# Attention on GpSimd and ScalarE: three small jobs of VectorE moved to other engines

## The chip, the cores and the metric

One Trainium2 chip, one core. The metric is the device time of one execution in microseconds, the median of the runs.

## The reference

A transformer block with adaptive layer norms on x of 8 batches x 512 tokens x 256, all in float32:

```
mod = (silu(c) @ wmod).reshape(8, 6, 1, 256);  sa, ca, ga, sb, cb, gb = mod[:, 0..5]
h = layernorm(x) * (1 + ca) + sa
Q = h @ Wq.T (16 heads of 16);  latent_k = h @ Wk_down.T;  latent_v = h @ Wv_down.T (64 wide)
logits = (Q q_to_latent) latent_k / 8, causal;  attn = softmax(logits)
x = x + ga * ((attn latent_v) v_up @ Wout.T)
h = layernorm(x) * (1 + cb) + sb
x = x + gb * (mixture of 16 experts, each on its 512 best tokens, + a shared expert)(h)
```

(ga and gb are first pushed to a magnitude of at least 0.25.) The change is in the attention half alone.

## The kernel before, in words

All five engines run programs of their own, written out by hand, and meet through semaphores. A product in float32 is made of three float32r products: each operand is split into an upper half (a rounded copy, names ending in h) and a lower half (the operand less the upper half, names ending in l).

The attention stage goes through 8 batches of 2 units each (NU = 16, unit u = 2b + c holds 8 heads of batch b), and each unit through 8 steps k, one per head. In step k of unit u TensorE makes a pair: the scores of head k of unit u into LB (main, L646, the matmuls of L656), interleaved with the scores of head k of unit u+1 into MB (maxima, L621, L633), which serve only to find the row maxima. VectorE reduces MB to row maxima NM (maxima, L1329, L1337), four blocks a head; TensorE may overwrite a block of MB only when VectorE has read it. ScalarE takes the exponentials P of LB in two parts (main, L1032 and L1034), and TensorE may overwrite LB only after them. GpSimd masks the diagonal of P (main, L1863). TensorE multiplies P with V (pv, L694) four heads at a time, in steps 4 and 5 for the first half of the unit and in steps 0 and 1 of the next unit for the second.

The negative maxima must be in place before the main scores of the same heads: they ride as two more rows of QS. In step 0 (for the upper four heads of unit u) and step 4 (for the lower four of unit u+1) TensorE transposes NM (put_max, L643), ScalarE copies it twice with a factor of -1, to NMh and NMf (put_max, L1010), VectorE subtracts NMl = NMf - NMh, 16x128 (put_max, L1341, semaphore d_nm), and ScalarE in step 1 or 5, behind its exponentials of that step and its copy of the PV result (store_heads, L1040), waits for d_nm and issues two DMAs that put NMh and NMl into QS (store_max, L1018, L1024).

Beside this, in fixed steps of the same loops, runs the work of other batches:

- the next batches' norm and projections. VectorE takes the statistics of batch b+2 (stats1, L1297, in step 0 of an odd unit) and the moments (moments, L1288: four aggregations, then var + eps and -mean, L1294 and L1295, on 128x4), GpSimd the power -1/2 and a product (moments, L1842, L1844 and L1846), ScalarE the scaled rows xh (scale1), TensorE their transpose (hT, steps 5 and 6), ScalarE hf = the shifted and scaled transpose (hT, L980, steps 5 and 6), VectorE the upper half hh (hT, L1316, cast of 128x512, steps 6 and 7), GpSimd the lower half hl (hT, L1853: one at the end of step 7, one before the mask of step 0 of the next unit). TensorE projects q and k from hh and hl in steps 1, 2, 6 and 7 of the even unit (qk, L577), ScalarE writes the upper and VectorE the lower half of the result (L996, L1326), and v in steps 2 and 3 of the odd unit.
- the finished batches. Batch b-1's (in even units b-2's second half) output projection on TensorE (outproj, L598), its product with the gate on VectorE (L1357) and its sum with X on GpSimd (outproj, L1882: end of step 7 of the odd unit, and behind the mask of step 0 of the even unit); then the second norm of batch b-2: statistics and moments on VectorE (stats2, moments2, steps 1 and 2 of the even unit), power on GpSimd (step 2), th on ScalarE (scale2, steps 3 and 4), two products and sums on GpSimd (shift2, L1891 and L1893, steps 4 and 6), transposes and score products.

In GpSimd's loop (L1915) the work of a step stands behind its mask. hf is a single buffer, which ScalarE refills only when hl is done (hl_done); the output projection in step 7 of the odd unit uses the bank of PSUM that the second hf of step 6 has to leave first.

Of the kernel before, what the change touches and what calls it, by code (L numbers as in the profile page):

```python
# [13 lines left out]
NB = 8  # L14
# [4 lines left out]
NU = 16  # L19
# [44 lines left out]
def block_program(nc, x, wq, wkd, wvd, q2l, vup, wo, gate, uw, ub, gw, gb, dw, db, sg, su, sd, ct, wmod,  # L64
# [55 lines left out]
    h2 = at("h2", 81024, [128, 2, 2, 512], F32R)  # L120
    halfc = at("halfc", 89216, [128, 4])
    st2, mv2 = at("st2", 89248, [128, 4, 6]), at("mv2", 89344, [128, 4, 2])
    rs2, nm2 = at("rs2", 89376, [128, 4]), at("nm2", 89408, [128, 4])
    for i_, n_ in enumerate(("wq", "wk", "wv")):
# [107 lines left out]
    a_sil, a_ht, a_cut, a_xt, a_score = (sem(n) for n in ("a_sil", "a_ht", "a_cut", "a_xt", "a_score"))  # L232
    a_sd, a_sc6 = sem("a_sd"), sem("a_sc6")

    (d_s, d_w, d_modT, d_mod, d_gate, d_mv1, d_hh, d_st, d_mx, d_nm, d_rec, d_tf, d_mv2, d_h2, d_lg) = (sem(n) for n in (
        "d_s", "d_w", "d_modT", "d_mod", "d_gate", "d_mv1", "d_hh", "d_st", "d_mx", "d_nm", "d_rec", "d_tf", "d_mv2",
        "d_h2", "d_lg"))
# [7 lines left out]
        "g_ks", "g_fill", "g_rs1", "g_P", "g_nf", "g_hn", "g_x2", "g_rs2", "g_h2", "g_ht"))  # L245
    g_sd = sem("g_sd")

# [723 lines left out]
    def scalar_program(e):  # L971
# [8 lines left out]
        def hT(b, c, name):  # L980
# [29 lines left out]
        def put_max(u, half):  # L1010
            e.wait_ge(p_mt, 2 * u + half + 1)
            if u:
                e.wait_ge(d_nm, 2 * u + half - 1)
                e.wait_ge(c_nm[half], 32 * u)
            e.activation(NMh[half][:], MB[0:16, 1280:1408], ACT.Copy, scale=-1.0)
            e.activation(NMf[half][:], MB[0:16, 1280:1408], ACT.Copy, scale=-1.0).then_inc(a_nm, 1)

        def store_max(u, half):  # L1018
            base = 64 * (u % 2)
            e.wait_ge(d_nm, 2 * u + half + 1)  # L1020
            if u >= 2:
# [123 lines left out]
        vproj(0, 1, "p1")  # L1145
        hT(1, 0, "p0")
        hT(1, 1, "p1")
        put_max(0, 0)
        store_max(0, 0)

        for u in range(NU):
            b, odd = u // 2, u % 2
            new, new2, old, old2 = b + 1 < NB, b + 2 < NB, 1 <= b, 2 <= b
            for k in range(8):
# [23 lines left out]
                else:  # L1178
# [94 lines left out]
    def vector_program(e):  # L1273
# [13 lines left out]

        def moments(stt, mvt, rst, nmt, done):  # L1288
# [12 lines left out]
        def moments1(b):  # L1301
            if b:
                e.wait_ge(a_xh, 2 * b)
            moments(st, mv, rs, nm1, d_mv1)

        def split_weight(n, src):
# [7 lines left out]
            e.tensor_tensor(l_, src, h_.bitcast(F32), ALU.subtract).then_inc(d_w, 1)  # L1314

        def hT(b, c):  # L1316
            e.wait_ge(a_hf, 2 * b + c + 1)
            if b:
                e.wait_ge(p_v, 2 * b)
            e.tensor_copy(hh[:, c, :], hf[:, c, :]).then_inc(d_hh, 1)  # L1320

# [7 lines left out]
        def maxima(u, k):  # L1329
            n = n_head(u, k)  # L1330
            for bank, blocks in ((2, (1,)), (1, (2, 0)), (0, (3,))):
# [7 lines left out]
                m.then_inc(d_mx, 1)  # L1339

        def put_max(u, half):  # L1341
            e.wait_ge(a_nm, 2 * u + half + 1)
            if u:
                e.wait_ge(c_nm[half], 32 * u)
            e.tensor_tensor(NMl[half][:], NMf[half][:], NMh[half][:].bitcast(F32), ALU.subtract).then_inc(d_nm, 1)

# [17 lines left out]
        def moments2(b):  # L1364
            if b:
                e.wait_ge(a_th, 2 * b)
            moments(st2, mv2, rs2, nm2, d_mv2)

# [90 lines left out]
        for c in range(2):  # L1459
            hT(0, c)  # L1460
            e.wait_ge(d_hh, c + 1)
            e.tensor_tensor(hl[:, c, :], hf[:, c, :], hh[:, c, :].bitcast(F32), ALU.subtract).then_inc(hl_done, 1)
# [10 lines left out]
        for k in range(8):  # L1473
            maxima(0, k)
            if k == 4:
                put_max(0, 0)
            if k in (4, 5):
                hT(1, k - 4)

        for u in range(NU):  # L1480
            b, odd = u // 2, u % 2
            new, new2, old, old2 = b + 1 < NB, b + 2 < NB, 1 <= b, 2 <= b
            for k in range(8):
                if u + 1 < NU:
                    maxima(u + 1, k)
                if k == 0:
                    put_max(u, 1)
                if k == 4 and u + 1 < NU:
                    put_max(u + 1, 0)

# [16 lines left out]
                else:  # L1507
# [324 lines left out]
    def pool_program(e):  # L1832
# [8 lines left out]

        def moments(b, ready, rst, nmt, done):  # L1842
# [41 lines left out]
        def shift2(b, half):  # L1884
# [8 lines left out]
            e.tensor_tensor(H2[:, ks, :], th[:, ks, :], BT[b % 2][:, 1:2, :].broadcast_to([128, 2, D]), ALU.add).then_inc(g_h2, 1)  # L1893

        kept(e.memset(halfc[:], -0.5))
        settled()
# [7 lines left out]
        settled()  # L1904
        moments(0, d_mv1, rs, nm1, g_rs1)

# [3 lines left out]
        m.then_inc(g_fill, 1)  # L1910
        moments(1, d_mv1, rs, nm1, g_rs1)
        hT(1, 0)
        hT(1, 1)

        for u in range(NU):  # L1915
            b, odd = u // 2, u % 2
            new2, old, old2 = b + 2 < NB, 1 <= b, 2 <= b
            for k in range(8):
                if not odd and k == 0 and 2 <= b + 1 < NB:

                    hT(b + 1, 1)
                main(u, k)
                if not odd:
# [150 lines left out]
```

## Time and profile before

| | us |
|---|---|
| median of 3 runs | 1156.96 (1151.46 to 1160.07) |
| the profiled execution | 1156.82 |
| its span | 1155.1 |
| TensorE's granted clock over the span | 0.978 |

Times in rows are microseconds from the start of the span unless marked ns. PE is TensorE, PEld its weight loads, DVE VectorE, ACT ScalarE, POOL GpSimd, SP SyncE; ACTq is a DMA issue in ScalarE's queue. A row of the timeline gives start, duration, engine, line, operation, out<-in, shape, count of merged instructions, and in brackets the idle time of the engine before it with what ended it. A duration reaches beyond the start of the next instruction, since an engine works in a pipeline; the step from start to start is what an instruction costs its engine.

### The profile page before, as it was taken

To read this page: it belongs to the slowest core of one execution; us is meant where nothing else is said; L and a number is where in the kernel's file an instruction comes from. 1 tells how busy PE (TensorE), PEld (TensorE's weight loads), DVE (VectorE), ACT (ScalarE), POOL (GpSimd) and SP (SyncE) were. 2 spreads that over 40 slices of the span, in tenths; PEclk is the share of its full clock that TensorE was granted. 3 is DMA by queue.
4 is the path that set the end of the run, shared out by engine and by line. 5 is a ranking of instruction groups with operands and counts; after the bars stand their busy time and mean duration, and the time that the engine had idled before them with its cause. 6 is when DMAs were issued, how large, how long until landed. Compare 5 with 4: busy or idle time off the path is not lost.

```text
span 1155.1 us, 21701 instructions
## 1 busy us (share of the span) xinstructions
PE 1112.3 (96%) x7482; PEld 865.4 (75%) x7482; DVE 861.1 (75%) x2213; ACT 594.1 (51%) x1083; POOL 633.1 (55%) x669
## 2 busy tenths in 40 slices
PE   9899999999999989999799999999999999999996
PEld 4555556656656668888688888888888888888886
DVE  4787888898898679889877677676777767777552
ACT  2356767877877653222253444544445444455441
POOL 4134566676675552232356656566565655666644
PEclk9789989999999999999999999999999999999998
DMA  7544557777767644876346554555545555455621
GB/s 198 91 99 101 115 120 182 178 147 179 187 131 177 208 160 109 270 220 164 98 139 165 134 131 123 155 140 134 134 127 153 134 143 136 119 152 132 168 58 19
DMA packets 100333, 165.44 MB, mean 143 GB/s; under 512 B 18424, under 2 KB 65016, under 8 KB 98176
## 3 DMA queue, kind: packets, MB, share of 16 engines
q1 hardware_dynamic: 83360, 137.04, 43.5%
q0 software_dynamic: 14336, 25.70, 11.5%
q10 hardware_dynamic: 2528, 1.32, 0.7%
q8 instruction: 60, 0.98, 0.4%
q14 instruction: 49, 0.40, 0.1%
HBM read 103.71 MB, written 34.11 MB: 119 GB/s over the span
## 4 chain that ended last, share of the span: by engine, by line
PE 63%; DVE 11%; issue 8%; POOL 8%; ACT 5%; DMA 3%; ACTq 1%; SPq 0%; DVEq 0%; POOLq 0%
PE MB L564 14%; PE LB L564 13%; PE LB L882 8%; PE MB L882 8%; PE UB L694 4%; PE LB L656 4%; PE UB L564 3%; PE XB L564 3%; POOL out_y L2001 3%; DVE junk L1337 2%; PE MB L633 2%; POOL XG L1966 1%; ACT P L1032 1%; ACT P L1034 1%; POOL HTl L1959 1%
## 5 line engine op out<-in xcount | busy, mean ns | idle before, releaser
L1959 POOL TENSOR_TENSOR HTl<-HF,HTh 128x512 fp32r<-128x512 f32 x156 | 217.6, 1401 | 207.7 <-ACT HTh L1095 207.4
L1337 DVE CUSTOM_DVE_ANT_0 junk<-MB,MK 128x256 bf16<-128x256 f32 (+3 forms) x512 | 218.6, 482 | 36.4 <-PE MB L633 35.5
L1863 POOL TENSOR_SCALAR_AFFINE_SELECT P<-P 128x256 f32<-128x256 f32 x256 | 101.3, 420 | 138.9 <-ACT P L1034 138.9
L2001 POOL DMA_INDIRECT out_y<-EO,IDX x64 | 108.7, 1699 | 75.7 <-DVE EO L1819 65.7
L1106 ACT ACTIVATE SIL<-LB,gbT 128x512 f32<-128x512 f32 x64 | 43.9, 686 | 191.8 <-PE LB L564 188.7
L1032 ACT ACTIVATE P<-LB 128x768 f32<-128x768 f32 x128 | 103.9, 812 | 73.4 <-PE LB L656 70.3
L633 PE MATMUL MB<-KS,QS 48*128 48x256 f32 (+3 forms) x512 | 132.8, 368 | 5.2 <-DVE NM L1337 3.4
L1095 ACT ACTIVATE HTh<-HF 128x512 fp32r<-128x512 f32 x156 | 97.8, 628 | 72.2 <-DVE HF L1709 72.2
L656 PE MATMUL LB<-QS,KS 50*128 50x256 f32 (+3 forms) x512 | 124.9, 358 | 3.5 <-ACT P L1032 2.6
L656 PEld LDWEIGHTS LB<-QS,KS 50*128 50x128 f32 x512 | 78.9, 190 | 50.2 <-issue 33.4
L633 PEld LDWEIGHTS MB<-KS,QS 48*128 48x128 f32 x512 | 81.7, 195 | 19.0 <-DVE NM L1337 12.7
L882 PE MATMUL LB<-WDh,HTh 128*128 128x256 f32 x320 | 93.3, 291 | 2.4 <-DVE tb L1723 2.3
L1709 DVE SCALAR_TENSOR_TENSOR HF<-MB,ubT,SIL 128x512 f32<-128x512 f32 x64 | 47.7, 745 | 63.8 <-PE MB L564 28.8
L1682 DVE TENSOR_TENSOR OH<-R,iotab 128x1024 bf16<-128x1024 bf16 x64 | 94.6, 1481 | 0.0
L882 PE MATMUL MB<-WDh,HTh 128*128 128x256 f32 x320 | 91.4, 286 | 0.0
L694 PE MATMUL UB<-P,V 128*32 128x512 f32 (+3 forms) x1024 | 86.5, 457 | 4.6 <-POOL P L1863 4.3
L882 PE MATMUL MB<-WDl,HTh 128*128 128x256 f32 x320 | 90.5, 283 | 0.0
L882 PE MATMUL MB<-WDh,HTl 128*128 128x256 f32 x320 | 90.5, 283 | 0.0
L882 PE MATMUL LB<-WDh,HTl 128*128 128x256 f32 x320 | 90.4, 282 | 0.0
L882 PE MATMUL LB<-WDl,HTh 128*128 128x256 f32 x320 | 90.3, 282 | 0.0
L1709 DVE SCALAR_TENSOR_TENSOR HF<-LB,ubT,SIL 128x512 f32<-128x512 f32 x64 | 47.7, 745 | 51.1 <-PE LB L564 47.0
L1966 POOL DMA_INDIRECT XG<-tab,IDX x64 | 63.8, 996 | 37.3 <-DVE IDX L1692 22.8
(316 smaller groups left out, 3028.1 us busy)
## 6 DMA issues: line engine op xcount, KB each, us to landing
WR<-in_gw SPq DMA_DIRECT2D x16, 1024.0 KB
WR<-in_uw SPq DMA_DIRECT2D x16, 1024.0 KB
WR<-in_dw SPq DMA_DIRECT2D x16, 1024.0 KB
QS<-ST SPq DMA_DIRECT2D x96, 128.0 KB, 3.7
KS<-ST SPq DMA_DIRECT2D x90, 128.0 KB, 4.6
hD<-h SPq DMA_DIRECT2D x8, 1024.0 KB, 6.1
XT<-hD SPq DMA_DIRECT2D x7, 1024.0 KB, 8.3
X<-in_x SPq DMA_DIRECT2D x8, 512.0 KB, 5.2
```

The lines of the kernel that those rows point to most:

```text
L564: m = e.matmul(ps, a(c), r(c), start=(i == 0), stop=(i == 5))
L633: m = e.matmul(MB[:, o:o + w], QS[base:base + 48, k, i * 128:(i + 1) * 128], KS[base:base + 48, k, 0:w], start=True, stop=True)
L656: m = e.matmul(LB[:, o:o + w], KS[base:base + 50, k, j * 128:(j + 1) * 128], QS[base:base + 50, k, 128 * j:512], start=True, stop=True)
L694: m = e.matmul(UB[32 * h:32 * h + 32, 128 * j:512], V[b % 2][:, j, 8 * c + 4 * g + h, :], P[(8 * u + 4 * g + h) % NP][:, o:o + w], start=( ...
L882: m = e.matmul(ps, a[:, slots[f], ts], r[:, f, :], start=(f == 0 and t_ == 0), stop=(f == len(slots) - 1 and t_ == 2), skip_group_check=True)
L1032: e.activation(P[n % NP][:, 512:1280], LB[:, 512:1280], ACT.Exp).then_inc(a_p, 1)
L1095: e.activation(HTh[:, slot, :], hf_of(n)[:], ACT.Copy).then_inc(a_ht, 1)
L1337: m = e.tensor_tensor_reduce(junk[:, o:o + w], MB[:, o:o + w], MK[:, 512 - w:512], 1.0, -3e38, ALU.add, ALU.max, NM[:, k // 4, 4 * (k % 4) ...
L1709: e.scalar_tensor_tensor(out=hf_of(n)[:], in0=up, scalar=bias, in1=sil_of(n)[:], op0=ALU.add, op1=ALU.mult).then_inc(d_hf, 1)
L1863: m = e.affine_select(out=dd, in_=dd, compare_op=ALU.is_ge, fill=0.0, base=0, pattern=[[0, 2], [1, 128]], channel_multiplier=-1)
L1959: e.tensor_tensor(HTl[:, slot, :], hf_of(n)[:], HTh[:, slot, :].bitcast(F32), ALU.subtract).then_inc(g_ht, 1)
L2001: e.indirect_dma_start(out=out2, out_offset=bass.IndirectOffsetOnAxis(ap=IDX[x_ % 3][:, q:q + 1], axis=0), in_=EO[:, q, :], in_offset=None ...
```

## The change

Three jobs leave VectorE's program:

- NMl = NMf - NMh (put_max) goes to GpSimd, with semaphore g_nm in place of d_nm. GpSimd does it at the head of step 1 (upper heads of unit u) and step 5 (lower heads of unit u+1), before the mask of that step, and for the first time behind the two hl of batch 1. ScalarE's store_max stays where it is, in steps 1 and 5, and now waits for g_nm.
- The upper half hh of the next h (hT) goes to ScalarE as a Copy activation (upper, semaphore a_hh), in steps 6 and 7 of odd units behind hf. Batch 0 keeps its cast on VectorE.
- The two small operations at the end of moments go to GpSimd's moments, as a product of the mean with a tile of -1 and a sum of the variance with a tile of eps, in front of the power. VectorE signals behind its last aggregation. For the last batch's second norm VectorE's own form stays.

```diff
         def upper(b, c):
+            e.wait_ge(a_hf, 2 * b + c + 1)
+            e.wait_ge(p_v, 2 * b)
+            e.activation(hh[:, c, :], hf[:, c, :], ACT.Copy).then_inc(a_hh, 1)
...
 scalar put_max / store_max
-                e.wait_ge(d_nm, 2 * u + half - 1)
+                e.wait_ge(g_nm, 2 * u + half - 1)
...
-            e.wait_ge(d_nm, 2 * u + half + 1)
+            e.wait_ge(g_nm, 2 * u + half + 1)
...
         hT(1, 0, "p0")
+        upper(1, 0)
         hT(1, 1, "p1")
+        upper(1, 1)
...
                     if k in (5, 6) and new2:
                         hT(b + 2, k - 5, ("hTa", "hTb")[k - 5])
+                    if k in (6, 7) and new2:
+                        upper(b + 2, k - 6)
...
 vector moments
-            kept(m)
-            settled()
-            e.tensor_scalar(rst[:], mvt[:, :, 1], EPS, None, ALU.add)
-            e.tensor_scalar(nmt[:], mvt[:, :, 0], -1.0, None, ALU.mult).then_inc(done, 1)
+            m.then_inc(done, 1)
...
 vector loops
-                if k == 0:
-                    put_max(u, 1)
-                if k == 4 and u + 1 < NU:
-                    put_max(u + 1, 0)
...
-                    if k in (6, 7) and new2:
-                        hT(b + 2, k - 6)
...
 gpsimd moments
+            e.tensor_tensor(nmt[:], mvt[:, :, 0], minus[:], ALU.mult)
+            kept(e.tensor_tensor(rst[:], mvt[:, :, 1], epsc[:], ALU.add))
+            settled()
             kept(e.tensor_tensor(rst[:], rst[:], halfc[:], ALU.pow))
...
 gpsimd hT
-            e.wait_ge(d_hh, 2 * b + c + 1)
+            e.wait_ge(a_hh, 2 * (b - 1) + c + 1)
...
+        def put_max(u, half):
+            e.wait_ge(a_nm, 2 * u + half + 1)
+            if u:
+                e.wait_ge(c_nm[half], 32 * u)
+            e.tensor_tensor(NMl[half][:], NMf[half][:], NMh[half][:].bitcast(F32), ALU.subtract).then_inc(g_nm, 1)
...
         hT(1, 0)
         hT(1, 1)
+        put_max(0, 0)
...
                 if not odd and k == 0 and 2 <= b + 1 < NB:
                     hT(b + 1, 1)
+                if k == 1:
+                    put_max(u, 1)
+                if k == 5 and u + 1 < NU:
+                    put_max(u + 1, 0)
                 main(u, k)
```

## Rows read from the trace of the kernel before

**Rows 1.** Busy time, share of the span and instructions of each engine.

```profile
PE 1112.3 (96%) x7482; PEld 865.4 (75%) x7482; DVE 861.1 (75%) x2213; ACT 594.1 (51%) x1083; POOL 633.1 (55%) x669
```

**Rows 2.** Stretches: bounds, length, busy time per engine, clock, DMA share, GB/s.

```profile
0.00:430.00 430.00, 405.81 (x2964) 249.16 (x2965) 345.54 (x1357) 284.42 (x543) 240.57 (x383) 0.95 0.62 150
...
212.64:256.74 44.10, 42.97 (x356) 27.10 (x356) 38.93 (x167) 34.02 (x66) 29.72 (x49) 1.00 0.73 167
```

**Rows 3.** Timeline of TensorE: first instruction of three pairs, and what follows each.

```profile
214.65 0.38 PE L656 MATMUL LB<-QS,KS 50*128 50x256 f32 x1
...
216.07 0.38 PE L564 MATMUL UB<-wvh,hh 128*128 128x256 f32 x1
...
240.32 0.38 PE L656 MATMUL LB<-QS,KS 50*128 50x256 f32 x1
...
241.54 0.73 PE L564 MATMUL XB<-h,GPh 128*128 128x512 f32 x2
...
250.46 0.38 PE L656 MATMUL LB<-QS,KS 50*128 50x256 f32 x1
...
251.30 0.51 PE L564 MATMUL XB<-hh,wkh 128*128 128x512 f32 x1
```

**Rows 4.** Groups by line from 75 to 410 us: busy, mean ns, idle before.

```profile
L1345 DVE TENSOR_TENSOR NMl<-NMf,NMh 16x128 fp32r<-16x128 f32 x29 | 13.5, 465 | 10.0 <-ACT NMf L1016 8.8
...
L1047 ACT ACTIVATE HNh<-nf 128x512 fp32r<-128x512 f32 x14 | 9.0, 642 | 1.1 <-POOL nf L1873 1.1
...
L1320 DVE CAST hh<-hf 128x512 fp32r<-128x512 f32 x12 | 5.1, 425 | 1.1 <-ACT hf L986 1.1
```

**Rows 5.** Timeline of VectorE, one batch.

```profile
234.18 0.72 DVE L1345 TENSOR_TENSOR NMl<-NMf,NMh 16x128 fp32r<-16x128 f32 x1
...
238.07 0.75 DVE L1285 BATCH_NORM_STATS2 st<-X 128x6 f32<-128x256 f32 x2 [0.26 <-POOL X L1882]
...
238.74 0.67 DVE L1326 SCALAR_TENSOR_TENSOR ST<-XB,ST 128x512 fp32r<-128x512 f32 x1
...
255.63 0.51 DVE L1345 TENSOR_TENSOR NMl<-NMf,NMh 16x128 fp32r<-16x128 f32 x1 [0.57 <-ACT NMf L1016]
```

**Rows 6.** Timeline of GpSimd, one batch.

```profile
231.41 0.77 POOL L1863 TENSOR_SCALAR_AFFINE_SELECT P<-P 128x256 f32<-128x256 f32 x2 [1.09 <-ACT P L1034]
...
232.23 1.28 POOL L1882 TENSOR_TENSOR X<-X,tf 128x512 f32<-128x512 f32 x1
...
233.48 2.57 POOL L1855 TENSOR_TENSOR hl<-hf,hh 128x512 fp32r<-128x512 f32 x2
...
236.74 1.30 POOL L1882 TENSOR_TENSOR X<-X,tf 128x512 f32<-128x512 f32 x1
...
242.80 0.20 POOL L1846 TENSOR_TENSOR nm<-nm,rs 128x4 f32<-128x4 f32 x1
...
246.17 1.29 POOL L1891 TENSOR_TENSOR th<-th,BT 128x512 f32<-128x512 f32 x1
...
247.54 1.28 POOL L1893 TENSOR_TENSOR H<-th,BT 128x512 f32<-128x512 f32 x1
```

**Rows 7.** Timeline of ScalarE, with its DMA issues, one batch.

```profile
226.05 1.36 ACTq L1024 DMA_DIRECT2D QS<-NMl  x1
...
229.36 0.79 ACT L986 ACTIVATE hf<-XB,modT 128x512 f32<-128x512 f32 x1
...
236.48 0.51 ACTq L1024 DMA_DIRECT2D QS<-NMh  x1
...
238.54 0.81 ACT L1032 ACTIVATE P<-LB 128x768 f32<-128x768 f32 x1
...
248.00 0.51 ACTq L1024 DMA_DIRECT2D QS<-NMh  x1
...
249.26 0.81 ACT L1032 ACTIVATE P<-LB 128x768 f32<-128x768 f32 x1 [0.64 <-PE LB L656]
```

**Rows 8.** The tile NMl: its DMAs from issue to landing.

```profile
DMA to landing us min/median/max: 1.9/2.8/5.6
```

More of the change, by code:

```diff
@@ L120, in block_program @@
     h2 = at("h2", 81024, [128, 2, 2, 512], F32R)
-    halfc = at("halfc", 89216, [128, 4])
+    halves, shifts = at("halves", 89216, [128, 8]), at("shifts", 89408, [128, 8])
+    halfc, minus = halves[:, 0:4], halves[:, 4:8]
+    nm2, epsc = shifts[:, 0:4], shifts[:, 4:8]
     st2, mv2 = at("st2", 89248, [128, 4, 6]), at("mv2", 89344, [128, 4, 2])
-    rs2, nm2 = at("rs2", 89376, [128, 4]), at("nm2", 89408, [128, 4])
+    rs2 = at("rs2", 89376, [128, 4])
     for i_, n_ in enumerate(("wq", "wk", "wv")):
@@ L232, in block_program @@
     a_sil, a_ht, a_cut, a_xt, a_score = (sem(n) for n in ("a_sil", "a_ht", "a_cut", "a_xt", "a_score"))
-    a_sd, a_sc6 = sem("a_sd"), sem("a_sc6")
-    (d_s, d_w, d_modT, d_mod, d_gate, d_mv1, d_hh, d_st, d_mx, d_nm, d_rec, d_tf, d_mv2, d_h2, d_lg) = (sem(n) for n in (
-        "d_s", "d_w", "d_modT", "d_mod", "d_gate", "d_mv1", "d_hh", "d_st", "d_mx", "d_nm", "d_rec", "d_tf", "d_mv2",
+    a_sd, a_sc6, a_hh = sem("a_sd"), sem("a_sc6"), sem("a_hh")
+    (d_s, d_w, d_modT, d_mod, d_gate, d_mv1, d_hh, d_st, d_mx, d_rec, d_tf, d_mv2, d_h2, d_lg) = (sem(n) for n in (
+        "d_s", "d_w", "d_modT", "d_mod", "d_gate", "d_mv1", "d_hh", "d_st", "d_mx", "d_rec", "d_tf", "d_mv2",
         "d_h2", "d_lg"))
@@ L245, in block_program @@
         "g_ks", "g_fill", "g_rs1", "g_P", "g_nf", "g_hn", "g_x2", "g_rs2", "g_h2", "g_ht"))
-    g_sd = sem("g_sd")
+    g_sd, g_nm = sem("g_sd"), sem("g_nm")
     g_own = sem("g_own")
@@ L987, in hT, with upper @@
                          scale=modT[:, 1, c, b:b + 1]).then_inc(a_hf, 1)
+        def upper(b, c):
+            e.wait_ge(a_hf, 2 * b + c + 1)
+            e.wait_ge(p_v, 2 * b)
+            e.activation(hh[:, c, :], hf[:, c, :], ACT.Copy).then_inc(a_hh, 1)
         def qk(b, c, kind, name):
@@ L1286, in stats, with moments @@
             kept(m)
-        def moments(stt, mvt, rst, nmt, done):
+        def moments(stt, mvt, done):
             settled()
@@ L1303, in moments1 @@
                 e.wait_ge(a_xh, 2 * b)
-            moments(st, mv, rs, nm1, d_mv1)
+            moments(st, mv, d_mv1)
         def split_weight(n, src):
@@ L1314, in split_weight @@
             e.tensor_tensor(l_, src, h_.bitcast(F32), ALU.subtract).then_inc(d_w, 1)
[L1316 to L1320, printed above, removed]
         def qk(b, c, kind, name):
@@ L1339, in maxima @@
                 m.then_inc(d_mx, 1)
[L1341 to L1345, printed above, removed]
         def inverses(u):
@@ L1366, in moments2 @@
                 e.wait_ge(a_th, 2 * b)
-            moments(st2, mv2, rs2, nm2, d_mv2)
+            moments(st2, mv2, d_mv2)
         def h2T(b, c, name):
@@ L1459, in vector_program @@
         for c in range(2):
-            hT(0, c)
+            e.wait_ge(a_hf, c + 1)
+            e.tensor_copy(hh[:, c, :], hf[:, c, :]).then_inc(d_hh, 1)
             e.wait_ge(d_hh, c + 1)
@@ L1474, in vector_program @@
             maxima(0, k)
[L1475 to L1478, printed above, removed]
         for u in range(NU):
@@ L1840, in settled, with moments @@
             e.wait_ge(g_own, own[0])
-        def moments(b, ready, rst, nmt, done):
+        def moments(b, ready, mvt, rst, nmt, done):
             e.wait_ge(ready, b + 1)
+            e.tensor_tensor(nmt[:], mvt[:, :, 0], minus[:], ALU.mult)
+            kept(e.tensor_tensor(rst[:], mvt[:, :, 1], epsc[:], ALU.add))
+            settled()
             kept(e.tensor_tensor(rst[:], rst[:], halfc[:], ALU.pow))
@@ L1893, in shift2 @@
             e.tensor_tensor(H2[:, ks, :], th[:, ks, :], BT[b % 2][:, 1:2, :].broadcast_to([128, 2, D]), ALU.add).then_inc(g_h2, 1)
+        e.memset(minus[:], -1.0)
+        e.memset(epsc[:], EPS)
         kept(e.memset(halfc[:], -0.5))
@@ L1904, in pool_program @@
         settled()
-        moments(0, d_mv1, rs, nm1, g_rs1)
+        moments(0, d_mv1, mv, rs, nm1, g_rs1)
         e.wait_ge(hl_done, 2)
@@ L1910, in pool_program @@
         m.then_inc(g_fill, 1)
-        moments(1, d_mv1, rs, nm1, g_rs1)
+        moments(1, d_mv1, mv, rs, nm1, g_rs1)
         hT(1, 0)
         hT(1, 1)
+        put_max(0, 0)
         for u in range(NU):
@@ L1928, in pool_program @@
                     if k == 2 and old2:
-                        moments(b - 2, d_mv2, rs2, nm2, g_rs2)
+                        moments(b - 2, d_mv2, mv2, rs2, nm2, g_rs2)
                     if k == (3 if u == NU - 2 else 7) and old:
@@ L1937, in pool_program @@
                     if k == 1 and new2:
-                        moments(b + 2, d_mv1, rs, nm1, g_rs1)
+                        moments(b + 2, d_mv1, mv, rs, nm1, g_rs1)
                     if k == 2 and old and u < NU - 1:
@@ L1944, in pool_program @@
                     if k == 5 and u == NU - 1:
-                        moments(NB - 2, d_mv2, rs2, nm2, g_rs2)
+                        moments(NB - 2, d_mv2, mv2, rs2, nm2, g_rs2)
                     if k == 7 and old and b + 1 < NB:
```

## The prediction, made before the changed kernel was run

> **What bounds the kernel now.** I read the busy shares first: TensorE is busy for 96% of the span, VectorE for 75%, so the bound looks settled, and isn't [rows 1]. Then the stretches: the attention stage, which alone is changed, lies in the first 430 us [rows 2]. From batch 2 on it repeats: one batch (an even unit and an odd unit, 16 steps) takes 44.1 us, with TensorE busy for 43.0, VectorE 38.9, ScalarE 34.0 and GpSimd 29.7 of them [rows 2]. I write e0 to e7 for the steps of an even unit and o0 to o7 for those of an odd one.
>
> TensorE's busy time has modelled ends, so I read the starts of its instructions instead. A step's pair (eight matmuls, the scores of this head and of the next unit's) takes 0.84 us when nothing holds it: from 250.46 to 251.30. The pair of o2 takes 1.42 (214.65 to 216.07) and that of e3 1.22 (240.32 to 241.54) [rows 3]. Added up so over the 16 pairs of one batch, the excess is some 2.8 us of 44.1. Of it some 1.8 has VectorE late with its row maxima (o2 0.58, e3 0.38, e4 0.37, the rest in four small pieces). The other 1.0 has ScalarE late, in o4 and o7. So what a perfect VectorE could give back is 1.8 us per batch; the rest of TensorE's time is its own work, its turnarounds, and ScalarE.
>
> **What is taken off VectorE.** Per batch: four subtractions for NMl, mean 0.465 us, with 0.34 us of idle time each before them (10.0 over 29) while VectorE waits for ScalarE's copy [rows 4]; two casts hh of 0.42 [rows 4]; four tiny operations of the norms of about 0.17 by the next tiny one on GpSimd of 0.20 [rows 6]. That is 4 x 0.80 + 2 x 0.42 + 4 x 0.1 (they overlap) = 4.4 us of 44.1. Only what meets one of the stalls counts. In the step before o2, VectorE waits 0.57 and works 0.51 on NMl at 255.63 [rows 5]; that row is the same place one batch later, 1.0 us ahead of a stall of 0.58: that stall goes, -0.58. ScalarE is the late one behind it and moves forward with it. e3 and e4 are for below.
>
> **What is added to ScalarE.** Two copies of 128x512 per batch. The nearest row is the copy HNh, 0.64 by its duration [rows 4], and some 0.5 from start to start. Both lie behind the second hf of o6 (229.36 [rows 7]), on which the output projection waits, so they don't delay TensorE there; but the exponentials of o7 come 0.5 later, and with them GpSimd's mask of o7, at 231.41 [rows 6]. From there GpSimd works without a pause: mask, X (232.23), two hl (233.48, 2.57), mask, X (236.74, 1.30) [rows 6]. TensorE's q projection wants the second hl at 236.28 and has it at 236.05 now; with 0.5 more it waits, +0.3.
>
> **What is added to GpSimd, and who waits for it.** The subtraction is 16x128. GpSimd's tiny operation takes 0.20 [rows 6], its 128x512 ones 1.29; a quarter of the row length is between: 0.45 taken, bounds 0.2 and 1.3. The busy time (four of these, four tiny ones, 2.6 us of an engine idle for 14) costs nothing. Its place does. ScalarE's step k=1 and k=5 issues the two DMAs of the negative maxima after waiting for the subtraction; a wait holds all of ScalarE behind it: the upper q copy, the next exponentials, and through them VectorE's lower q and TensorE's next scores.
>
> Wait A, step e1. ScalarE reaches the DMAs at 236.48 [rows 7]. VectorE has delivered at 234.18 + 0.72 [rows 5]. GpSimd delivers only when X of 236.74 is through: 238.04 + 0.45 = 238.5, a wait of 2.0 us, and 2.4 with the delay of the copies. Behind it: exponentials of e2, now 238.54 [rows 7], and VectorE's lower q, now 238.74 [rows 5], from which its maxima of e2 run on to 240.97, already 0.38 late for e3. This chain has no slack: the end of e3 moves by about 2.0. VectorE's relief at 234.18 is lost here, since it then waits for ScalarE (and before that for X, at 238.07 [rows 5]).
>
> Wait B, step e5. ScalarE is there at 248.00 [rows 7]. GpSimd has the mask of e4, then th and H from 246.17 to 248.82 [rows 6], then the subtraction: 249.3, a wait of 1.3. The exponentials of e6, now 249.26 with a first half that ends at 250.07 [rows 7], come at 250.5; e7 on TensorE wants that half at 250.46 [rows 3], so 0.4 is slack and 0.9 is paid. The norm's scale for the second layer norm comes from GpSimd later than now too (its two tiny operations stand ahead of the power, and the masks before it are late by A), another 0.2.
>
> Wait C, step o5: the split of HN (1.3) stands ahead of the subtraction on GpSimd. By the same addition ScalarE waits 0.4, ahead of a DMA issue that is itself long (1.36 at 226.05 [rows 7]) and of hf, whose chain ends in e0: +0.4. In o1 GpSimd is done in time, and no wait arises.
>
> Per batch: -0.58 + 0.3 + 2.0 + 0.9 + 0.2 + 0.4 = +3.2, less 0.1 to 0.2 for the small pieces in o6 and e4: +3.1. Batches 2 to 6 have all of this: 5 x 3.1 = 15.5. Batches 0 and 1 have no X and no second norm, so GpSimd is in time, and I take 1 us of relief for each (the 0.58 and one lower piece). Batch 7 has no hl at its start, so A nearly vanishes, B and C stay: +1. The profiled execution took 1156.8 us in all, by chance the median of the runs shown (1157.0). Sum: 1156.8 + 15.5 - 2 + 1 = 1171.3; I say 1171.
>
> Bounds. With the subtraction at 0.2, A, B and C are each 0.25 shorter: 5 x 0.75 = 3.8 less, 1167. At 1.3 they are 0.85 longer: 5 x 2.5 = 13 more, 1184. The copies at 0.4 or 0.64 instead of 0.5 move it by 1. The small sums cost nothing unless they delay the scale by more than the 0.25 that VectorE gains.
>
> The Trainium skill (Perfetto Trace Analysis, Optimizing Scalar/DVE Operations) says that work of a saturated VectorE may go to ScalarE or even GpSimd, and warns that GpSimd and VectorE share a read port of SBUF, so that a move between these two might not help. If each moved subtraction had to sit out one VectorE operation of 0.67, A, B and C would grow by that: 5 x 3 x 0.67 = 10 more, 1181. No row shows GpSimd in that place; its masks and subtractions in this stage keep their 0.77 and 1.29 beside a busy VectorE, which speaks against it.
>
> **Rivals.**
> (1) Faster: VectorE is what TensorE waits for, and the waits of ScalarE are absorbed. Then the 1.8 us per batch come back, 5 x 1.8 + 2 = 11 less: 1146. For it: VectorE is at 88% in the stage [rows 2] and its lateness is the commonest stall. Against it: the DMAs are issued at 236.48, and X ends after 238.0; ScalarE would have to reach them 2 us later than now. It decides if e3's exponentials had over 2 us of slack; by [rows 3, 7] the first half ends at 239.35 for a pair at 240.32, 1.0.
> (2) About equal: only half of A and B reaches TensorE, because relief and slack add up where I took none, and the batch loses 1.0: 1156.8 + 5 - 1 = 1161.
> (3) Worse: beside the waits, the DMAs issued later land too late for e4 and o0, where the scores need them. The DMAs of e1 would be issued 2.4 us later and those of e5 3.5, TensorE itself being 2.0 and 3.1 later where it wants them; a landing takes 2.8 us in the median and up to 5.6 [rows 8], so at the long end e4 and o0 wait, another 1 to 2 us per batch, 1179.
> That the change doesn't do what it says is no rival: the instructions only change engines.
>
> **How the numbers follow.** What a measurement here can tell from no change is about 1%, 11.6 us. My forecast 0.5, rival 1 0.12, rival 2 0.22, rival 3 0.16. Of my forecast some 0.08 ends below 1168.5. So faster by over 1%: 0.10 (of rival 1's 0.12 a little stays within 1%); within 1%: 0.30; slower by over 1%: 0.60. Range 1152 to 1182: it takes in rivals 2 and 3 and the shorter and longer subtraction, and leaves out rival 1 and the end at 1184.
>
> **What would show it.** Right: a batch takes about 47.2 us; the subtraction of e1 starts right behind GpSimd's X, that of e5 right behind H; ScalarE's DMA issues in e1 and e5 follow it directly; the pair of o2 takes 0.84; those of e3 and e7 take over 2; the q projection waits shortly for hl; VectorE's busy time in a batch is down to some 36. Wrong: a batch under 44 us, with e3 and e4 near 0.84; or ScalarE working on behind an unserved DMA wait, which takes the ground from A and B; or the loss in DMA landings, which would be rival 3.

## The result, and the profile after

The changed kernel takes 1173.58 us (median of 4 runs, 1173.05 to 1177.57), the kernel before, in runs between them, 1157.68 (1151.46 to 1160.07): a ratio of 1.0159, 95% interval 1.0121 to 1.0196. It is slower, and the prediction (1171, range 1152 to 1182) holds. The profiled execution of after is the longest of its four, 1177.57 us with a span of 1175.8; it lies 20.8 above that of before (1156.8), where the medians differ by 15.9. So terms per batch are read from the traces, and totals from the ratios.

The page of after, busy time of each engine (busy us, share of the span, instructions), for [rows 1]:

```profile
span 1175.8 us, 21703 instructions
...
PE 1122.1 (95%) x7482; PEld 869.7 (74%) x7482; DVE 842.7 (72%) x2137; ACT 600.1 (51%) x1097; POOL 648.5 (55%) x733
```

VectorE lost 18.4 us of work, GpSimd gained 15.4 and ScalarE 6.0, as the diff says. TensorE has the same 7482 instructions and is 9.8 us longer busy: the same work took it longer. That is the first hint of something that the prediction doesn't have.

The same by stretches: one batch (bounds, length, busy time of PE, PEld, DVE, ACT, POOL, granted clock, DMA share, GB/s), and three pieces of 2 us inside it. It runs from step o0 to the next o0, that of [rows 2] from o1 to o1; either is one whole period:

```profile
213.70:261.50 47.80, 44.08 (x358) 27.62 (x356) 36.87 (x156) 34.74 (x69) 31.82 (x57) 0.96 0.64 156
246.00:248.00 2.00, 1.75 (x8) 0.90 (x7) 2.00 (x12) 1.39 (x3) 1.21 (x5) 0.85 0.00 0
248.00:250.00 2.00, 2.00 (x6) 1.40 (x5) 1.54 (x8) 1.08 (x3) 1.80 (x4) 0.50 0.27 90
250.00:252.00 2.00, 1.99 (x15) 0.98 (x17) 0.98 (x5) 1.04 (x3) 0.00 (x0) 0.80 0.71 172
```

A batch takes 47.8 us instead of 44.1, with VectorE at 36.9 of them. The clock over the batch is 0.96 instead of 1.00, and from 248 to 250 it is 0.50, the lower of its two levels (1.2 of 2.4 GHz).

GpSimd in e1 and e5 (start us, us, engine, line, operation, tiles), for [rows 6]:

```profile
236.42 1.28 POOL L1881 TENSOR_TENSOR X<-X,tf 128x512 f32<-128x512 f32 x1
237.67 2.52 POOL L1847 TENSOR_TENSOR hl<-hf,hh 128x512 fp32r<-128x512 f32 x2
...
240.88 1.28 POOL L1881 TENSOR_TENSOR X<-X,tf 128x512 f32<-128x512 f32 x1
242.13 0.45 POOL L1864 TENSOR_TENSOR NMl<-NMf,NMh 16x128 fp32r<-16x128 f32 x1
...
254.71 1.28 POOL L1892 TENSOR_TENSOR H<-th,BT 128x512 f32<-128x512 f32 x1
255.95 0.45 POOL L1864 TENSOR_TENSOR NMl<-NMf,NMh 16x128 fp32r<-16x128 f32 x1
```

ScalarE and its DMA issues (ACTq) in the same steps, for [rows 7]:

```profile
240.27 0.61 ACT L1048 ACTIVATE Us<-UB 128x512 f32<-128x512 f32 x1
242.61 0.51 ACTq L1032 DMA_DIRECT2D QS<-NMh  x1
243.15 0.81 ACTq L1032 DMA_DIRECT2D QS<-NMl  x1
244.08 0.60 ACT L1004 ACTIVATE ST<-XB 128x512 fp32r<-128x512 f32 x1 [3.20 <-issue]
244.57 0.81 ACT L1040 ACTIVATE P<-LB 128x768 f32<-128x768 f32 x1
...
255.20 0.61 ACT L1048 ACTIVATE Us<-UB 128x512 f32<-128x512 f32 x1
256.43 0.52 ACTq L1032 DMA_DIRECT2D QS<-NMh  x1
...
257.69 0.81 ACT L1040 ACTIVATE P<-LB 128x768 f32<-128x768 f32 x1 [1.89 <-issue]
```

Read the two together. The subtraction starts as soon as X ends (242.13), the DMA issue as soon as the subtraction ends (242.58, 242.61), and the q copy and the exponentials stand behind the two issues. The DMAs of e5 do the same behind H. The label "issue" hides it: this view puts the pause down to nothing that it knows, since the waiting instruction is a DMA issue and not the copy. Before, the first DMA issue came with the start of Us (236.48 [rows 7], Us at 236.50), and nothing stood still.

TensorE, first instructions of what matters, for [rows 3] (o2 at 219.37, then e3 from 245.43, e7 from 258.56):

```profile
219.37 0.38 PE L658 MATMUL LB<-QS,KS 50*128 50x256 f32 x1
...
220.21 0.39 PE L566 MATMUL UB<-wvh,hh 128*128 128x256 f32 x1
...
243.93 0.40 PE L566 MATMUL UB<-hh,wkl 128*128 128x512 f32 x1
245.43 0.38 PE L658 MATMUL LB<-QS,KS 50*128 50x256 f32 x1 [1.10 <-ACT P L1040]
...
247.58 1.22 PE L566 MATMUL XB<-h,GPh 128*128 128x512 f32 x2
248.60 0.63 PE L566 MATMUL XB<-h,GPl 128*128 128x512 f32 x1
...
250.44 0.53 PE L658 MATMUL LB<-QS,KS 50*128 50x256 f32 x1
...
257.27 0.40 PE L566 MATMUL UB<-hh,wql 128*128 128x512 f32 x1
258.56 0.39 PE L658 MATMUL LB<-QS,KS 50*128 50x256 f32 x1 [0.89 <-ACT P L1040]
```

The pair of o2 takes 0.84: its stall is gone. The pair of e3 waits 1.10 for the exponentials and is then held by VectorE's maxima, so that the score product of the finished batch (XB<-h,GPh and GPl) starts at 247.58. That product then takes 2.86 us (247.58 to 250.44); in the batch of [rows 3] it took 1.59, by the chain of waits. Here lies the piece with the clock at 0.50. It isn't this batch alone: in all four batches that have the product behind an e3 with wait A (3 to 6) it takes 2.76 to 2.86.

Last the chain of waits in this stretch (start us, us, what):

```profile
240.91 1.25 POOL X L1881
242.16 0.42 POOL NMl L1864
242.59 0.02 issue
242.61 0.51 ACTq L1032
...
243.15 0.81 ACTq L1032
...
244.08 0.61 ACT ST L1004
...
244.71 0.05 DVE ST L1329
...
245.31 0.42 DVE junk L1340
```

In the kernel before, the chain of this stretch is TensorE's own work without a break. Now it runs X on GpSimd, subtraction, DMA issue, copy, maxima: wait A is in the chain of the whole kernel.

### The profile page after: what moved, and what is told of

It is laid out like the page before. It is cut to its first block, busy times and chain, and to the rows that moved or that the text cites. A ratio compares the mean times of both kernels' runs of the same rounds, so it can differ in the third digit from the quotient of the medians.

```text
span 1175.8 us, 21703 instructions
## 1 busy us (share of the span) xinstructions
PE 1122.1 (95%) x7482; PEld 869.7 (74%) x7482; DVE 842.7 (72%) x2137; ACT 600.1 (51%) x1097; POOL 648.5 (55%) x733
## 4 chain that ended last, share of the span: by engine, by line
PE 59%; POOL 11%; DVE 9%; issue 9%; ACT 6%; DMA 2%; ACTq 2%; SPq 0%; DVEq 0%; POOLq 0%
PE MB L566 15%; PE LB L566 15%; PE LB L884 8%; PE MB L884 8%; PE UB L696 3%; PE LB L658 2%; DVE junk L1340 2%; ACT P L1040 2%; POOL P L1855 2%; POOL out_y L2007 2%; ACTq L1032 2%; ACT P L1042 1%; PE UB L566 1%; PE XB L566 1%; POOL X L1881 1%
## 5 line engine op out<-in xcount | busy, mean ns | idle before, releaser
L1855 POOL TENSOR_SCALAR_AFFINE_SELECT P<-P 128x256 f32<-128x256 f32 x256 | 98.6, 409 | 160.7 <-ACT P L1042 160.7
L658 PE MATMUL LB<-QS,KS 50*128 50x256 f32 (+3 forms) x512 | 130.9, 370 | 14.1 <-ACT P L1040 12.9
L1114 ACT ACTIVATE SIL<-LB,gbT 128x512 f32<-128x512 f32 x64 | 43.9, 686 | 190.9 <-PE LB L566 185.7
L658 PEld LDWEIGHTS LB<-QS,KS 50*128 50x128 f32 x512 | 82.5, 198 | 64.2 <-issue 35.0
L696 PE MATMUL UB<-P,V 128*32 128x512 f32 (+3 forms) x1024 | 90.2, 473 | 5.4 <-POOL P L1855 5.2
L1697 DVE SCALAR_TENSOR_TENSOR HF<-MB,ubT,SIL 128x512 f32<-128x512 f32 x64 | 47.7, 745 | 64.1 <-PE MB L566 28.8
L1697 DVE SCALAR_TENSOR_TENSOR HF<-LB,ubT,SIL 128x512 f32<-128x512 f32 x64 | 47.7, 746 | 51.2 <-PE LB L566 48.8
```

Of the source, the lines that this page charges most:

```text
L658: m = e.matmul(LB[:, o:o + w], KS[base:base + 50, k, j * 128:(j + 1) * 128], QS[base:base + 50, k, 128 * j:512], start=True, stop=True)
L696: m = e.matmul(UB[32 * h:32 * h + 32, 128 * j:512], V[b % 2][:, j, 8 * c + 4 * g + h, :], P[(8 * u + 4 * g + h) % NP][:, o:o + w], start=( ...
```

## The experiments

Theory: what is lost is the place of the subtraction in GpSimd's order (waits A and B), and the lower clock that these waits bring with them. The rivals were that GpSimd's load as such costs, that the copies or the sums do, that DMA landings do, and later that a gain seen came from an issue at another time. Each run's comparison is with the kernel before on the same chip (median 1156.50 beside the first four, 1157.03 beside the next four, 1157.53 beside the last four). "Batch" is the period of batches 3 to 5 in the profile, from the transpose of the maxima in e0 to the same one a batch later: 44.1 in before, 47.7 to 48.3 in after. (Batches 2 and 6 are left out: in before they take 47.1, with a stretch of low clock, and 42.9.)

**1. Only the subtraction back on VectorE** (all else as after):

```diff
 vector loops
+                if k == 0:
+                    put_max(u, 1)
+                if k == 4 and u + 1 < NU:
+                    put_max(u + 1, 0)
 gpsimd loops
-                if k == 1:
-                    put_max(u, 1)
-                if k == 5 and u + 1 < NU:
-                    put_max(u + 1, 0)
```

> The changed kernel with the subtraction NMl put back on VectorE where it was; the copies hh stay on ScalarE and the small sums on GpSimd. Theory (the waits of ScalarE for GpSimd's subtraction carry the loss): the waits A and B vanish, a batch takes 44 to 44.5 us, and the time is 1156 to 1161 us, within 0.4% of the kernel before; the q projection still waits 0.3 us for hl. Rival (the copies on ScalarE carry it): 1166 us or more.

1162.19 us (1153.93 to 1170.52), ratio 1.0037 [1.0003, 1.0071]; batch 44.6. Of the 1.6% that after loses, 1.2% go with the subtraction. The rest of the change isn't free as it stands here, 0.4% in the median, 1.2 us above the range that was expected.

**2. Only the subtraction on GpSimd** (all else as before; the mirror of 1):

> The kernel before with only the subtraction NMl moved to GpSimd, in the places of the change; hh and the small sums stay on VectorE. Theory of the waits: nearly the whole loss, 1168 to 1174 us, with ScalarE's DMA issues in e1 and e5 directly behind GpSimd's subtraction. Rival (the copies on ScalarE or the small sums carry it): 1155 to 1161 us.

1175.94 us (1173.37 to 1176.20), ratio 1.0147 [1.0098, 1.0196], above the range expected by 1.9 us; batches 46.1 to 47.3. The DMA is issued at 242.82, behind a subtraction that starts at 242.34 right behind X (241.09, 1.29). The subtraction alone makes the loss. The batch of 46.1 is the one in which the score product takes 1.58; in the two of 47.2 and 47.3 it takes 2.55 and 2.85.

**3. The two DMA issues one step later** on ScalarE, the subtraction where after has it:

```diff
-                if k == 1:
+                if k == 2:
                     store_max(u, 1)
-                if k == 5 and u + 1 < NU:
+                if k == 6 and u + 1 < NU:
                     store_max(u + 1, 0)
```

> The changed kernel with ScalarE's two DMA issues one step later (steps 2 and 6, behind the exponentials of that step), so that it doesn't stand waiting for GpSimd; GpSimd's places are unchanged and the DMAs land as late as now or later. Theory (what costs is that ScalarE is held, not that the negative maxima come late): 1148 to 1162 us, e3 and e7 without their long waits. Rival (the late DMAs are what TensorE waits for): 1172 us or more, with waits of TensorE for the DMA in e4 and o0.

1155.34 us (1152.80 to 1160.91), ratio 0.9999 [0.9970, 1.0028]; batches 42.6 to 43.5, 43.1 in the mean, the shortest of all kernels here. So the work on GpSimd costs nothing; ScalarE's standing before it does. But the total is only that of before. The waits of the first batches (engine, line, what it waited for: us in total, times, longest), from 85 to 112 us:

```profile
PEld LB L658 <- DMA QS<-NMl: 5.6, 2, 4.9
```

In the first batches the DMA issued a step later lands too late, and the scores wait 4.9 us once: the first batch takes 48.8 instead of 45.7. This is rival 3 of the prediction, shown as a mechanism, but in the start, and only with an issue a whole step later. A second loss stands at the end of the attention stage:

```profile
380.00:390.00 10.00, 9.99 (x63) 5.47 (x64) 2.39 (x4) 6.21 (x12) 4.74 (x8) 0.83 0.14 45
```

From 380 to 410 us the clock is at 0.83 to 0.93, where before has 1.00 in that batch. At the last transpose of the maxima this kernel is 4.7 us ahead of before (380.84 for 385.55), at the last pair of scores 0.4 behind (412.38 for 411.94). Why the clock falls there isn't shown.

**4. Filler work on TensorE in e2**, so that it isn't idle while it waits in e3. The ten products go to the bank that the k projection right behind them overwrites, so nothing reads them. They take 1.29 us:

```diff
+                    if k == 2 and new and old2:
+                        ps = spare("k0")
+                        for _ in range(10):
+                            e.matmul(ps[:, 0:256], W["wo"][0][:, 0, 0:128], W["wo"][0][:, 0, :], start=True, stop=True)
```

> The changed kernel with ten further products of 256 columns (about 1.1 us) on TensorE in step e2 of batches 2 to 6, ahead of the k projection, into a bank that this projection then overwrites; they leave the output as it is and fill most of the time in which TensorE would wait for ScalarE in e3. Theory (part of the loss is TensorE's clock, granted at 0.50 for some 3 us after the waits of e3, so that the score product takes 2.86 instead of 1.58 us): the granted clock stays at 1.00 there, the score product takes 1.6 us, and the time falls by 4 to 7 us to 1167 to 1170, although work was added. Rival (the clock's fall is free, or comes from something else): the same time or more, 1174 to 1179 us.

1172.21 us (1169.21 to 1175.77), ratio 1.0122 [1.0068, 1.0175]. The same two places by stretches:

```profile
246.00:248.00 2.00, 2.00 (x9) 1.22 (x11) 2.00 (x10) 1.07 (x3) 1.66 (x5) 1.00 0.02 8
...
258.00:260.00 2.00, 2.00 (x8) 1.20 (x8) 1.02 (x3) 0.80 (x2) 1.92 (x2) 0.50 0.79 210
```

In place it does what was expected: the clock stays at 1.00, and the score product takes 1.60 (246.28 to 247.88) instead of 2.86; in all four batches it takes 1.58 to 1.60. The batches are 46.5 to 47.4, some 1.0 shorter. But in this trace the clock falls 10 us later instead, behind wait B. In total 4 to 7 us less than after were expected; the medians, taken on two chips, differ by 1.4, the ratios (1.0122 for 1.0159) by 4.3, and the intervals overlap. So the fall of the clock in e3 is shown to come with the idle time there, and the 1.27 us with the clock; its share of the total isn't shown by this run.

**5. The subtraction one step earlier on GpSimd**, in step 0 ahead of the mask and in step 4 behind it. The edit holds for odd units too. Wait A (in e1) goes with the first of the two places, B (in e5) and C (in o5) with the second:

```diff
-                if k == 1:
+                if k == 0:
                     put_max(u, 1)
-                if k == 5 and u + 1 < NU:
-                    put_max(u + 1, 0)
                 main(u, k)
+                if k == 4 and u + 1 < NU:
+                    put_max(u + 1, 0)
```

> The changed kernel with GpSimd's subtractions earlier in its own queue: the upper one in step 0, behind the second hl and ahead of the mask, the lower one in step 4, behind the mask and ahead of th and H (even units) or the split of HN (odd units). ScalarE's places are unchanged. Theory: B and C vanish and A shrinks to 0.4 us; a batch takes 43 to 44 us, 1149 to 1156 us. Rival (VectorE's relief is worth nothing): 1158 us or more.

1151.41 us (1148.39 to 1157.05, 12 runs), ratio 0.9959 [0.9937, 0.9982]: faster than before by its interval, as was expected; run 12 says how far such an interval carries. GpSimd, then the same batch by stretches:

```profile
230.19 2.54 POOL L1847 TENSOR_TENSOR hl<-hf,hh 128x512 fp32r<-128x512 f32 x2
232.67 0.45 POOL L1864 TENSOR_TENSOR NMl<-NMf,NMh 16x128 fp32r<-16x128 f32 x1
...
242.60 0.77 POOL L1855 TENSOR_SCALAR_AFFINE_SELECT P<-P 128x256 f32<-128x256 f32 x2 [1.66 <-ACT P L1042]
243.33 0.45 POOL L1864 TENSOR_TENSOR NMl<-NMf,NMh 16x128 fp32r<-16x128 f32 x1
243.75 1.28 POOL L1890 TENSOR_TENSOR th<-th,BT 128x512 f32<-128x512 f32 x1
```

```profile
208.40:252.10 43.70, 42.44 (x359) 26.68 (x355) 36.80 (x156) 35.07 (x71) 31.92 (x57) 1.00 0.72 169
```

The subtraction ends at 233.12 and 243.78. ScalarE is at its Us copy at 232.90 and 244.90, and issues the DMAs at 233.15 and 244.77: of wait A 0.25 is left, of B nothing. VectorE does as little (36.80) and GpSimd as much (31.92) as in after, the clock is 1.00, and the batch takes 43.7. The same instructions on the same engines, in another order, are worth 2.0% (1.0159 against 0.9959).

**6 and 7. Each of the two places alone**: the edit of 5 in step 0 only, and in step 4 only.

> The same with the upper subtraction alone moved ahead (into step 0); the lower one stays at the head of step 5. Theory: A and the fall of the clock go, about 3 of 4.9 us a batch, B stays: 1155 to 1162 us, clock at 1.00 behind e3.

> The same with the lower subtraction alone moved ahead (into step 4); the upper one stays at the head of step 1. Theory: B and C go, about 1.4 us a batch, A and the fall of the clock stay: 1164 to 1170 us.

Step 0 alone (A away, B and C stay): 1162.89 us (1160.27 to 1167.62), ratio 1.0048 [1.0021, 1.0075], batches 45.3 to 46.1; the time is 0.9 above the range expected. As was expected, the clock doesn't fall behind e3: the score product takes 1.58 to 1.60. Step 4 alone (B and C away, A stays): 1164.48 us (1156.85 to 1171.11), ratio 1.0049 [1.0022, 1.0076]. By the ratios, taking away A gives 1.11% and B with C 1.10%, together 2.2% for 2.0% of both: within the intervals the two are about equal and add up. The prediction had A at 2.0 us a batch and B with C at 1.5 (0.9, 0.2 and 0.4); with the clock's 1.27, which the traces put to A, A should have been worth more than twice the other. By the batches of the profiles it is about twice (43.4 to 43.7 with neither wait, 45.3 to 46.1 with B and C, 47.3 to 48.4 with A), but by the medians it isn't, and why not is open. The profile of the second is of its longest run, 1171.11; behind wait A it shows what else a wait can set off:

```profile
246.00:248.00 2.00, 2.00 (x8) 1.18 (x10) 1.85 (x9) 1.08 (x3) 1.84 (x5) 0.73 0.17 58
248.00:250.00 2.00, 2.00 (x13) 1.09 (x17) 1.59 (x7) 1.77 (x5) 0.18 (x1) 0.50 0.74 195
250.00:252.00 2.00, 2.00 (x16) 0.40 (x8) 1.10 (x4) 1.38 (x5) 1.82 (x4) 0.50 1.01 140
252.00:254.00 2.00, 2.00 (x16) 1.04 (x9) 0.65 (x3) 0.25 (x1) 1.85 (x2) 0.56 0.68 163
```

Here the clock stays low for some 7 us and not for 3 as in after, and the batches take 47.3 to 48.4 though wait B is gone. The stretch of low clock varies from run to run, and with it the time (14 us between the shortest and longest run, with a granted clock of 0.979 and 0.969 over the whole).

Nor does a wait of one length always bring it. At e7 of one batch in run 6 TensorE waits 1.30 us for the exponentials, and the clock stays at 1.00; at e7 in the filler run it waits 1.31, and the clock falls to 0.50.

**8. Subtraction early in e4, and in e1 of the even units (from batch 2 on) the DMA issue one step later** instead of the earlier subtraction:

```diff
-                if k == 1:
+                if k == (2 if old2 and not odd else 1):
                     store_max(u, 1)
```

> The changed kernel with the lower subtraction in step 4 on GpSimd, as before, and ScalarE's DMA issues for the upper one in step 2 instead of 1, in the even units from batch 2 on alone, so that the first batches keep their early DMAs. Theory: no wait of ScalarE is left, a batch takes 43 us, and the time is 1146 to 1152 us, faster than both kernels. Rival (relief of VectorE is worth nothing): 1156 us or more.

1151.65 us (1147.06 to 1154.41, 11 runs), ratio 0.9946 [0.9925, 0.9967]; batches 43.2 to 44.1. The subtraction of e1 ends at 236.77, ScalarE issues the DMA at 237.05, and nothing waits. Wait A can be taken away from either end, by an earlier subtraction or by a later issue, with the same result; leaving batches 0 and 1 alone avoids the late landing of run 3. Both 5 and 8 are below both kernels, and the two intervals overlap. It isn't only the clock: of the runs with a granted clock of 0.978 to 0.982, the median is 1152.2 in run 5 (9 runs), 1152.1 in run 8 (7) and 1156.2 in before beside them (14).

**9. Only the subtraction on GpSimd, in the places of 5** (all else as before):

> The kernel before with only the subtraction NMl on GpSimd, in the early places (step 0 ahead of the mask, step 4 ahead of th and H or the split of HN); hh and the small sums stay on VectorE. Theory (VectorE's relief ahead of o2, e3 and e4 is what is gained, and NMl is the largest part of it): 1148 to 1154 us, a batch at 43 to 43.6 us. Rival (the gain of the early version comes from hh and the sums): 1156 us or more.

1154.57 us (1152.39 to 1156.42), ratio 0.9981 [0.9960, 1.0002]; batches 43.5 to 43.9. The time lies between the range of the theory and that of the rival, so neither is borne out. The relief by the subtraction alone is some 0.2%, at the limit of what can be told.

**10 and 11. The copies alone, and the small sums alone** (before, with that one part of the diff):

> The kernel before with only the copies hh moved to ScalarE. Theory: q projection 0.3 us later a batch, VectorE's relief lies where TensorE doesn't wait for it: 1156 to 1161 us, no gain. Rival: the 0.8 us of VectorE come back, 1151 to 1154 us.

> The kernel before with only the small sums of the moments moved to GpSimd. Theory: 0.1 to 0.3 us a batch in either direction, 1154 to 1160 us, not to be told from the kernel before.

Copies: 1158.25 us (1153.06 to 1164.14), ratio 1.0005 [0.9978, 1.0031], batch 44.5. Sums: 1160.81 us (1153.98 to 1165.28), 0.8 above the range expected, ratio 1.0024 [0.9998, 1.0051], batches 44.3 to 44.8. Neither is a gain by itself, and the batch is 0.2 to 0.7 longer with each; they don't explain the loss. Run 5, which has both beside the subtraction, isn't told apart from run 9, which has neither: the intervals overlap and the batches are 43.4 to 43.7 and 43.5 to 43.9.

**12. Only the later DMA issue of 8, on the kernel before**, to see if the later issue is a gain by itself:

> The kernel before with nothing moved from VectorE; only ScalarE's DMA issues for the upper maxima one step later, in the even units from batch 2 on. Theory (the gain of the version with this edit comes from the relief of VectorE, and the later store only avoids wait A): 1155 to 1160 us, as before. Rival (the later issue is itself the gain): 1150 to 1153 us.

1161.25 us (1152.99 to 1163.79), ratio 1.0039 [1.0012, 1.0065]; steady batches 44.0 to 44.2. No gain, so that of 8 needs the relief. But it is 1.25 us above the range expected, and there is no reason in the program for 0.4% more. Two rows, the first of before, the second of this run:

```profile
120.00:140.00 20.00, 18.94 (x172) 12.41 (x171) 16.24 (x76) 16.25 (x33) 10.40 (x19) 1.00 0.46 98
```

```profile
120.00:140.00 20.00, 19.16 (x119) 11.72 (x117) 13.33 (x59) 12.77 (x28) 9.33 (x17) 0.68 0.47 100
```

At 120 to 140 us the edit changes nothing (batch 1 comes before it sets in), yet the clock is at 0.68, TensorE gets 119 instructions done instead of 172, and products of twelve matmuls take 2.86 us (128.53, 132.86). This batch takes 50.9 us, in before 44.9. What stands ahead of it is the same in both, the first of before, the second of this run:

```profile
124.16 0.38 PE L633 MATMUL MB<-KS,QS 48*128 48x256 f32 x1 [0.58 <-DVE NM L1337]
```

```profile
126.44 0.38 PE L633 MATMUL MB<-KS,QS 48*128 48x256 f32 x1 [0.59 <-DVE NM L1337]
```

The same instruction waits the same time, and a wait of 0.25 and 0.24 follows; only in run 12 does the clock fall behind it. Before has such a piece elsewhere, a clock of 0.83 at 140 to 160.

The granted clock is on record for every run. In run 12 the two runs at 0.983 and 0.984 took 1152.99 and 1153.46 us, the ten at 0.974 to 0.977 took 1159.95 to 1163.79. In the 35 of before beside it, the four at 0.984 or more took 1148.56 to 1152.91, the five at 0.973 or less 1160.25 to 1163.54. So the scatter within one kernel goes with the clock, some 8 to 10 us for each 0.01 (an estimate, a line through these runs), and the stretches are enough for much of ratios of 0.2 to 0.4%, as in runs 1, 11 and 12. An interval here holds the noise of the runs, but a gain of 0.4 or 0.5% is no larger than this 0.4% without a reason; for runs 5 and 8 the comparison at equal clock and the shorter batches stand beside it. What sets a stretch off isn't shown, nor how often it comes, with one profile per kernel.

## Why the prediction was right

**What bounds the kernel**: right. VectorE's lateness was worth little; relieved by 2 us of work per batch, the batch got 0.4 to 0.7 shorter in run 5 (43.4 to 43.7 for 44.1) and 1.0 in the mean in run 3 (43.1), whose batches are the shortest, not the 1.8 of rival 1.

**The terms per batch**, from the trace of after:

| step | predicted | measured | from |
|---|---|---|---|
| o2, stall gone | -0.58 | -0.58 | 219.37 to 220.21: 0.84 |
| q projection waits for hl | +0.3 | +0.2 | its first matmul at 240.25, one hl ending at 240.19 |
| wait A at the end of e3 | +2.0 | +2.1 | the pair starts 1.15 later and takes 2.15 instead of 1.22 |
| wait B at e7 | +0.9 | +0.97 | 1.29 between 257.27 and 258.56, 0.32 before |
| scale of the second norm later, wait C | +0.2, +0.4 | +0.26 in o0 | 0.61 for the long DMA issue there, C itself 0.2 |
| e4, o6, o7 | -0.1 to -0.2 | -0.43 | -0.14, -0.16, -0.13 |
| lower clock behind e3 | none | +1.27 | 2.86 for 1.59 |
| sum | +3.1 | +3.8 | period 47.8 for 44.1: +3.7 |

**The subtraction on GpSimd**: 0.45 taken, 0.45 measured, in each of the rows above. **Wait A itself**: ScalarE is at Us, where it issued before, at 240.27, and issues at 242.61: 2.3, for 2.4 predicted. **Wait B**: 255.20 to 256.43, 1.2 for 1.3. The two waits were the right two, in the right places, behind the right instructions (X, H). Of the signs of being right, one came only in part: the pair of e3 takes over 2 (2.15), that of e7 takes 0.91, with the wait of 0.89 ahead of it.

**What failed**: three things, inside a total that came out right.
- The step "this chain has no slack: the end of e3 moves by about 2.0" stops one step too early. TensorE, having waited, works on at half its clock for 3 us, and the price of A is 2.1 + 1.27. The prediction took the product behind e3 at its price of before.
- Wait C, +0.4, was mostly covered. ScalarE waited 0.2, and the DMA issue that takes 1.36 at this place in [rows 7] took 0.61 here, so that hf came no later. The sizes of the small reliefs (e4, o6, o7) were low by 0.2 to 0.3.
- "I take 1 us of relief for each" of batches 0 and 1 didn't come: they are 0.6 longer and 0.4 shorter. What came instead is a first unit that starts 1.7 us earlier, which the prediction doesn't have. That the two are nearly the same size is luck, and so is part of the total: the missing price of the clock (1.27 a batch) is partly made up by wait C and the small reliefs, and by the low clock that before has in batch 2.

Against the total: the first unit starts 1.7 us earlier than in before, and from there the batches, even unit to even unit, are longer by 0.6, -0.4, 1.2, 4.0, 4.2, 3.6 and 6.4, and the rest by some 2. The 1.2 is small only because before has a stretch of low clock in that batch. Together this is the +20.3 us at the last transpose of the maxima (405.86 for 385.55), of the 20.7 by which the span is longer. The 6.4 is of the batch from 333 to 382 us. Three stretches of it; before has a clock of 1.00 throughout this batch:

```profile
340.00:345.00 5.00, 3.57 (x13) 1.80 (x12) 4.14 (x21) 3.58 (x6) 2.75 (x6) 0.80 0.17 61
345.00:350.00 5.00, 5.00 (x22) 2.50 (x24) 3.22 (x14) 3.23 (x8) 1.71 (x7) 0.50 0.78 157
350.00:355.00 5.00, 5.00 (x45) 2.39 (x38) 2.53 (x12) 2.33 (x4) 3.67 (x5) 0.68 0.04 7
```

The same wait A, and behind it a low clock that lasts some 10 us instead of 3 (0.50 in every 2 us from 344 to 352), and a batch longer by 2.7 us more than the 3.7 of the one in the table. Only one of the four executions has a trace, so that this is why the profiled one is 4 us above the three others isn't shown, but it is of the size. By the medians the forecast is 2.6 low.

**Rivals.** 1 (faster, absorbed): refuted by wait A standing in the chain, and by run 2. 2 (half absorbed): refuted, A and B are both paid nearly in full. 3 (late landings): not here; TensorE's weight loads wait 2.0 us in all for the DMAs of NMl in after and 1.8 before (75 to 410 us). It is real with an issue a whole step later (run 3). The warning of the Trainium skill (Perfetto Trace Analysis, Optimizing Scalar/DVE Operations), that GpSimd and VectorE share a read port, would by the prediction's working have made it 1181. This trace doesn't bear it out for this operation: the subtraction takes 0.44 to 0.46 at all 29 places from 75 to 410 us, also beside a busy VectorE.

## What to carry to other kernels

When an operation moves to an engine with time to spare, don't ask how busy that engine is but what stands ahead of the operation in its order, and what stands behind the instruction that waits for it, DMA issues first: the same subtraction on the same engine, alone, cost 1.5% behind X and H, and nothing that can be told (0.2% less, at the limit) one step ahead. If a queue's wait shows up, both ends can be moved, the producer earlier or the issue later, but the issue only where its landing has slack. A gap in TensorE of 1 to 2 us may cost more than its length, so price the work right behind it at the lower clock too, as an upper bound: the fall came behind some such gaps here and not behind others.

## What was not expected of the hardware

- The granted clock of TensorE falls to its lower level behind e3: 0.85, 0.50 and 0.80 in the three pieces from 246 to 252 us, where TensorE had waited 1.10 and then some 0.5 in pieces; the whole batch has it busy for 44.1 of 47.8 us. With filler in the wait the clock stays at 1.00 there (run 4). The Trainium skill (TensorE: Matmul & The Clock Gate, Part 1) says that there are only two levels, set by how busy the array has been lately. The traces agree on the two levels: whole pieces at 1.00 or 0.50, values between them where a piece holds a change.
- The low stretch behind the same wait lasts about 3 us in one batch of after, some 10 in another, and 7 in run 7, and such stretches come without any edit there (batch 1 in run 12, batch 2 in before itself). The runs of one kernel lie up to 17 us apart (run 1), and 10 to 12 runs give an interval of 0.2 to 0.35% to either side.
- Issuing the DMA of NMl holds ScalarE for 0.61, 0.81 or 1.36 us by the rows, for the same bytes; what makes it long isn't shown.
- The subtraction of 16x128 takes GpSimd 0.45 us each time, and VectorE 0.465 in the mean, but 0.35 in the median (0.28 to 1.22; 0.51 and 0.72 are the ones in [rows 5]). For so small a tile the move costs the operation 0.1 us by the medians.
